# A perceiver block with a mixture of experts: the order of sixteen small matmuls in the attention's value products

## Chip, cores and metric

The kernel runs on one core of one Trainium2 chip, as one program. The metric is device time in microseconds of that core, the median of three runs. The profile is of one further execution of the same program.

## What is computed

One block of a perceiver: cross attention of 8 x 64 tokens onto 8 x 512 context rows, then causal self attention that is applied twice with a convolution between, then a mixture of 14 experts with two chosen per token. The part that matters here is the self attention:

```
qkv = x @ Wqkv_w.T + Wqkv_b
q, k, v = (qkv[:, :, 0], qkv[:, :, 1], qkv[:, :, 2])   # 16 heads of 32
ctx = _causal_attn(q, k, v)
conv_out = conv1d(ctx, conv_w, width 3) + conv_b
q2 = conv_out.reshape(b, s, 16, 32)
ctx2 = _causal_attn(q2, k, v)
out = ctx2 @ out_w.T + out_b
```

with _causal_attn: softmax of masked q k / sqrt(32), times v. There are 8 batches of 64 tokens, 512 features.

## The kernel before

The 512 tokens are cut into NT = 4 tiles of P = 128 rows, each of two batches (j = 0, 1) of S = 64 tokens. Each engine has its program written out by hand, and semaphores order them; nothing is moved by a scheduler. TensorE (the function under block.tensor) goes through the cross attention, then through eight attention steps m = 0 to 7: m = 0 to 3 are the four tiles in the first attention, m = 4 to 7 the same tiles in the second. In a step, `scores(m, half)` (line 1588) multiplies q and k per head, DVE takes the maximum and subtracts (lines 1070, 1071), ACT takes the exponential (581), DVE sums it (1078), POOL multiplies by the reciprocal (771), `values(m)` (1597) turns the probabilities on TensorE, ACT copies them to prT (589), and `outputs(m, w)` (1619) multiplies them with v. DVE's `take_out` (1092) adds the bias of v, writes the result and raises o_ready. Between these stand fills: projections of q, k and v (1535 to 1545) and the convolution (1555), placed by the table SLOTS. In the loop, step m runs `scores(m)`, `values(m - 1)`, `outputs(m - 1, 0)` and `outputs(m - 1, 1)`, with a fill after most of them. The last two steps stand after the loop in a list of their own (lines 1708 to 1746), mixed with the output projection `out_project` (1637), the turning of the normalised rows for the gate `turn_gate` (1384 by way of a helper), the gate's logits (1653), counts (1666, 1667) and the dispatch to the experts (1702). Then the experts' stage follows (1767 to 1769 for the first layer, 1790 for the second).

`outputs(m, w)` is called 16 times. One call makes 16 matmuls in fp32. H = 16 heads of DH = 32 features; HR = P // DH = 4. The head is h = 4(2 hp + w) + r. The stationary operand is v of one head and one batch: 64 rows (the key tokens, S) by 32 columns (the head's features). The moving operand is prT, the turned probabilities: 64 rows (key tokens) by 64 columns (query tokens). The result, 32 partitions by 64, goes to the partitions 32 r to 32 r + 31 of one PSUM bank, PO, at a column that follows from w, hp and j. So r says which strip of 32 columns of the array, and which 32 partitions of the bank, a matmul uses. w picks the rows of the array, the lower or the upper 64, and is the same within a call. With w = 0 a call waits for the turned probabilities (pT_ready) and until DVE has taken what the bank held before (o_ready); with w = 1 it waits for the matmuls of w = 0 (o_psum). The last matmul of each call raises o_psum; `take_out(m)` waits for both calls.

Of the kernel before, what the change touches and what calls it, by code (L numbers as in the profile page):

```python
# [31 lines left out]
HR = P // DH  # L32
# [16 lines left out]
def perceiver_kernel(nc, t, out):  # L49

    ctx = ExitStack()
    with ctx:
# [1325 lines left out]
        def _(pe):  # L1378
# [223 lines left out]
            def outputs(m, w):  # L1602

                n, u = m % NT, m % 2
                if w == 0:
                    pe.wait_ge(pT_ready, 2 * m + 2)
                    if m:
                        pe.wait_ge(o_ready, 2 * m)
                    if m < NT:
                        pe.wait_ge(vx_in[n], 32)  # L1610
                else:
                    pe.wait_ge(o_psum, 2 * m + 1)
                for hp in range(2):
                    for j in range(2):
                        for r in range(HR):
                            h = HR * (2 * hp + w) + r
                            v = vN if w == j else vX
                            at = 2 * P * w + P * hp + S * j
                            ins = mm(PO[DH * r:DH * (r + 1), at:at + S],
                                     v[S * w:S * (w + 1), n, DH * h:DH * (h + 1)],  # L1620
                                     prT[S * w:S * (w + 1), u, 4 * (r % 2) + 2 * (r // 2) + hp, S * j:S * (j + 1)],
                                     start=True, stop=True)
                ins.then_inc(o_psum, 1)
# [55 lines left out]
            for m in range(2 * NT - 2):  # L1679
                scores(m, 0)  # L1680
                fill(SLOTS[m][0])
                scores(m, 1)
                fill(SLOTS[m][1])
                if m:
                    values(m - 1)
                fill(SLOTS[m][2])
                if m:
                    outputs(m - 1, 0)
                fill(SLOTS[m][3])
                if m:  # L1690
                    outputs(m - 1, 1)
# [20 lines left out]
            values(before - 1)  # L1712
            fill(SLOTS[before][1])
            outputs(before - 1, 0)
            fill(SLOTS[before][2])
            turn_gate(0)
# [171 lines left out]
```

## Time and profile before

| | |
|---|---|
| median of 3 runs | 463.60 us (463.52 to 463.69) |
| profiled execution | 463.69 us |
| its span, first to last instruction | 461.9 us |
| TensorE matmuls busy | 434.2 us, 94% |
| VectorE busy | 277.5 us, 60% |
| ScalarE busy | 162.6 us, 35% |
| GpSimd busy | 50.4 us, 11% |
| mean granted clock of TensorE | 0.985 |

PE is TensorE's matmul side, PEld its weight loads, DVE VectorE, ACT ScalarE, POOL GpSimd. Each fp32 matmul appears as two matmul records and two weight loads. The end of a matmul record is modelled from its start: records of small matmuls overlap in the trace, and what counts is how far apart they start, or how long a group of them takes together. A record's own duration holds a fixed latency that lies beside the next ones. The granted clock is a share of 2.4 GHz. The chain of work that ended last is the profile's path back from the last instruction, with the time each piece added to it.

### The profile page before, as it was taken

The numbers are of one execution on the slowest core, as the hardware profiler recorded it, in microseconds if no ns is written. First come the engines' busy times: TensorE is split into PE (matmuls) and PEld (weight loads), VectorE is DVE, ScalarE is ACT, GpSimd is POOL, SyncE is SP. The second block draws the span as 40 slices with busy tenths as digits, with TensorE's granted clock in tenths as the row PEclk, the third lists the DMA queues.
The fourth block names the chain that finished last, engine by engine and source line by source line (L and its number), as shares of the span: only waits on it lengthen the run. The fifth ranks groups of instructions, "written<-read, shape, count | busy, mean of one in ns | idle before, by whom it ended". The sixth has DMA issues, their size and how long they took to land.

```text
span 461.9 us, 8060 instructions
## 1 busy us (share of the span) xinstructions
PE 434.2 (94%) x3103; PEld 312.0 (68%) x3112; DVE 277.5 (60%) x552; ACT 162.6 (35%) x316; POOL 50.4 (11%) x59
## 2 busy tenths in 40 slices
PE   1999999999999999999998999999999999999990
PEld 1666566688888899978567766666666656666660
DVE  5759697663544223389668866654456664445637
ACT  4335234114232114432326332455433355543100
POOL 1300000004221011110302300000000000000064
PEclk9999999999999999998989999999999999999996
DMA  7998794007999666005224669999999999984453
GB/s 263 406 390 324 261 415 178 1 1 270 405 406 403 247 241 241 1 3 203 81 89 178 199 203 376 352 325 339 335 338 362 380 323 341 340 320 142 171 151 122
DMA packets 52383, 116.95 MB, mean 253 GB/s; under 512 B 4835, under 2 KB 4851, under 8 KB 52353
## 3 DMA queue, kind: packets, MB, share of 16 engines
q1 hardware_dynamic: 25984, 67.12, 38.3%
q10 hardware_dynamic: 24800, 44.62, 27.5%
q0 software_dynamic: 1568, 4.79, 3.2%
q8 instruction: 21, 0.34, 0.3%
q14 instruction: 10, 0.07, 0.0%
HBM read 93.98 MB, written 21.50 MB: 250 GB/s over the span
## 4 chain that ended last, share of the span: by engine, by line
PE 87%; DVE 6%; DMA 2%; issue 2%; ACT 1%; POOL 1%; DVEq 0%; ACTq 0%; POOLq 0%
PE banks L1790 19%; PE banks L1555 10%; PE banks L1767 6%; PE banks L1769 6%; PE banks L1768 5%; PE banks L1416 4%; PE banks L1418 3%; PE banks L1403 3%; PE banks L1455 3%; PE banks L1417 3%; PE banks L1384 3%; PE banks L1637 3%; PE banks L1779 2%; PE banks L1588 2%; PE banks L1535 2%; PE banks L1597 2%
## 5 line engine op out<-in xcount | busy, mean ns | idle before, releaser
L1790 PE MATMUL banks<-w,A 128*128 128x512 f32 x208 | 91.6, 592 | 0.0
L670 ACT ACTIVATE A<-banks,b_sb 128x128 f32<-128x128 f32 x112 | 30.5, 384 | 111.0 <-issue 61.1
L1790 PEld LDWEIGHTS banks<-w,A 128*128 128x128 f32 x208 | 38.5, 190 | 43.1 <-issue 43.0
L1288 DVE COPY A<-banks 128x512 f32<-128x512 f32 x28 | 18.0, 686 | 66.9 <-PE banks L1769 66.7
L1216 DVE TENSOR_TENSOR w_lo<-w,w_hi 128x1024 fp32r<-128x1024 f32 x48 | 55.4, 1216 | 0.0
L603 ACT ACTIVATE w_hi<-w 128x1024 fp32r<-128x1024 f32 x48 | 47.3, 1095 | 0.8 <-ACT A L670 0.8
L1555 PE MATMUL banks<-A,w 128*128 128x128 f32 x384 | 46.6, 277 | 0.0
L1555 PEld LDWEIGHTS banks<-A,w 128*128 128x128 f32 x384 | 44.1, 192 | 0.8
L1767 PE MATMUL banks<-w_hi,xr 128*128 128x512 f32 x100 | 40.1, 401 | 0.6 <-DVE xr L1233 0.6
L1768 PE MATMUL banks<-w_lo,xr 128*128 128x512 f32 x104 | 40.5, 389 | 0.0
L1769 PE MATMUL banks<-w_hi,xr 128*128 128x512 f32 x100 | 39.0, 390 | 0.0
L809 POOL DMA_INDIRECT wqkv<-rows_dram,slot_i x8 | 7.6, 955 | 182.9 <-DMA rows_dram<-A 180.8
L771 POOL TENSOR_TENSOR A<-A,hrec 128x1024 f32<-128x1024 f32 x8 | 16.5, 2060 | 91.4 <-DVE hrec L1079 91.4
L1416 PE MATMUL banks<-w_lo,A2r 128*128 128x512 f32 x52 | 22.4, 430 | 2.1 <-DVE A2r L937 2.1
L1070 DVE TENSOR_REDUCE hmax<-banks 128x16 f32<-128x1024 f32 x8 | 9.8, 1222 | 22.0 <-PE banks L1588 22.0
L1768 PEld LDWEIGHTS banks<-w_lo,xr 128*128 128x128 f32 x104 | 19.6, 188 | 3.6
L1767 PEld LDWEIGHTS banks<-w_hi,xr 128*128 128x128 f32 x100 | 18.8, 188 | 4.2 <-DVE xr L1233 0.9
L581 ACT ACTIVATE A<-w 128x1024 f32<-128x1024 f32 x8 | 8.5, 1058 | 37.3 <-DVE w L1071 37.3
L1769 PEld LDWEIGHTS banks<-w_hi,xr 128*128 128x128 f32 x100 | 18.8, 188 | 4.0
L1418 PE MATMUL banks<-w_lo,A2r 128*128 128x512 f32 x52 | 21.1, 406 | 0.0
L1417 PE MATMUL banks<-w_lo,A2r 128*128 128x512 f32 x52 | 21.0, 404 | 0.0
L1535 PE MATMUL banks<-c_hi,w_lo 128*128 128x256 f32 x64 | 18.5, 289 | 0.5 <-DVE A2r L977 0.5
(288 smaller groups left out, 741.4 us busy)
## 6 DMA issues: line engine op xcount, KB each, us to landing
w<-in_w SPq DMA_DIRECT2D x12, 2048.0 KB, 10.4
w<-in_w ACTq DMA_DIRECT2D x12, 2048.0 KB, 10.4
rows_dram<-att ACTq DMA_DIRECT2D x1, 14592.0 KB, 42.8
A<-in_ctxT SPq DMA_DIRECT2D x8, 1024.0 KB, 10.3
A<-in_ctx SPq DMA_DIRECT2D x8, 1024.0 KB, 9.4
w<-in_w SPq DMA_DIRECT2D x6, 1024.0 KB, 5.8
rows_dram<-A ACTq DMA_DIRECT2D x13, 256.0 KB, 3.4
w<-in_wlT SPq DMA_DIRECT2D x3, 1024.0 KB, 15.1
```

The lines of the kernel that those rows point to most:

```text
L603: nc.scalar.activation(w1_hi[:, u, k * F:(k + 1) * F], w1[:, u, k * F:(k + 1) * F], ACT.Copy).then_inc(hi_ready, 1)
L670: ins = nc.scalar.activation(hT[:, u, f, :], HT[f // 4][:, tile(f % 4)], ACT.Gelu, bias=b1_sb[:, u, f:f + 1])
L1216: nc.vector.tensor_tensor(w1_lo[:, u, part], w1[:, u, part], w1_hi[:, u, part].bitcast(F32), ALU.subtract).then_inc(lo_ready, 1)
L1416: mm(Z[n][:, :], high[:, k, :], wl_hi[:, at, :], start=(part == 0 and k == 0), stop=False)
L1417: mm(Z[n][:, :], high[:, k, :], wl_lo[:, at, :], start=False, stop=False)
L1418: ins = mm(Z[n][:, :], low[:, k, :], wl_hi[:, at, :], start=False, stop=(part == 2 and k == KT - 1))
L1535: mm(onto, w_hi, c_hi[:, k, tokens], start=(k == 0), stop=False)
L1555: ins = mm(bank[:, tile(f)].rearrange("p (b s) -> p b s", b=2), conv[:, KT * tap + k, tile(f)], oT[:, k, 2 * n:2 * n + 2, tap:tap + S], st ...
L1767: mm(HP[u][c][:, :], xr[:, 0, u, k, :], high[:, at], start=(i == 0), stop=False)
L1768: mm(HP[u][c][:, :], xr[:, 0, u, k, :], low[:, at], start=False, stop=False)
L1769: ins = mm(HP[u][c][:, :], xr[:, 1, u, k, :], high[:, at], start=False, stop=(i == KT - 1))
L1790: ins = mm(YP[:, :], hT[:, u, f, :], w2[:, u, f * D:(f + 1) * D], start=(f == 0), stop=(f == FT - 1))
```

## The change

In `outputs` the three loops over hp, j and r are put in another order. Before, hp is outermost and r innermost; after, r is outermost, then hp, then j. The 16 matmuls, their operands, where each writes, the waits ahead of them and the semaphore that the last one raises are the same; every product is complete in one matmul (start and stop are both set), so no sum depends on the order.

```
-                for hp in range(2):
-                    for j in range(2):
-                        for r in range(HR):
-                            h = HR * (2 * hp + w) + r
+                for r in range(HR):
+                    for hp in range(2):
+                        h = HR * (2 * hp + w) + r
+                        for j in range(2):
                             v = vN if w == j else vX
                             at = 2 * P * w + P * hp + S * j
                             ins = mm(PO[DH * r:DH * (r + 1), at:at + S],
```

The order of r within a call is thus 0 1 2 3, four times over, before, and 0 0 0 0 1 1 1 1 2 2 2 2 3 3 3 3 after. (hp, j) runs through (0,0), (0,1), (1,0), (1,1), each for four matmuls before, and anew for each r after. No other engine's program is touched, and a call stands at the same place among TensorE's other work. The two places that the prediction speaks of, with each row an instruction or a run of equal ones (operands by the program's names, stationary x moving columns):

On TensorE, step 1 in the loop: its two calls (line 1619) between pieces of the convolution (1555) and of the next step.

```order
L1555 MATMUL banks<-A2,w1 128x128 [waits conv_in,pads_ready,o_ready,fill_taken]
L1555 MATMUL banks<-A2,w1 128x128 x11
L1619 MATMUL banks<-A2,A1 32x64 [waits vx_in1,o_ready,pT_ready]
L1619 MATMUL banks<-A2,A1 32x64 x15
L1555 MATMUL banks<-A2,w1 128x128 [waits conv_in,pads_ready,o_ready,fill_taken]
L1555 MATMUL banks<-A2,w1 128x128 x11
L1619 MATMUL banks<-A2,A1 32x64 [waits o_psum]
L1619 MATMUL banks<-A2,A1 32x64 x15
L1577 MATMUL banks<-causal_bf,ident_bf 128x512 [waits fill_taken,sub_ready]
```

These rows are the same before and after: what moves is which strip each of the sixteen uses, which the rows don't print.

On TensorE, after the loop: step 7's two calls, between an output projection and the gate, with what waits behind them.

```order
L1637 MATMUL banks<-w2,cT 128x512 x3
L1619 MATMUL banks<-A2,A1 32x64 [waits o_ready,pT_ready]
L1619 MATMUL banks<-A2,A1 32x64 x15
L1619 MATMUL banks<-A2,A1 32x64 [waits o_psum]
L1619 MATMUL banks<-A2,A1 32x64 x15
L1653 MATMUL banks<-gate,cT 128x14 [waits lg_taken,sub_ready,cT_ready]
L1653 MATMUL banks<-gate,cT 128x14 x3
L1384 MATMUL banks<-ident,cn 128x128 [waits cT_ready,normed]
```

Here too the rows stay where they are, and only the order inside the two groups of sixteen is another.

## Rows read from the trace of the kernel before

**Rows 1.** The page's parts 1 and 2: TensorE busy, and granted clock.
```profile
PE 434.2 (94%) x3103; PEld 312.0 (68%) x3112; DVE 277.5 (60%) x552; ACT 162.6 (35%) x316; POOL 50.4 (11%) x59
...
PEclk9999999999999999998989999999999999999996
```
**Rows 2.** TensorE's waits from 130 to 262 us: total, times, longest.
```profile
PE banks L1702 <- DVE att L1138: 1.1, 1, 1.1
PE banks L1767 <- DVE xr L1233: 0.8, 1, 0.8
PE banks L1577 <- issue: 0.8, 5, 0.2
PE banks L1577 <- DVE lgc L1107: 0.5, 1, 0.5
PE banks L1384 <- DVE cn L837: 0.5, 1, 0.5
PE banks L1597 <- POOL A L771: 0.3, 1, 0.3
```
**Rows 3.** The chain that ended last: start us, us added, what.
```profile
149.93 0.58 PE banks L1619 x32
...
233.37 3.51 PE banks L1637 x4
...
236.97 1.82 PE banks L1637 x4
```
**Rows 4.** Line 1619, all records: duration ns min/median/max, first and last start, form.
```profile
L1619 PEld LDWEIGHTS banks<-A x512: 102/107/107, 137.4 to 230.8; 64*32 64x32 f32 x171
L1619 PE MATMUL banks<-A x512: 216/216/241, 137.4 to 230.9; 64*32 64x64 f32 x171
...
L1619 PE MATMUL banks<-A 64*32 64x64 f32 x512 | 10.4, 219 | 0.3
```
**Rows 5.** Timeline of one call, cut at 149.92 (both), 149.96 and 150.30.
```profile
149.86 0.26 PE L1619 MATMUL banks<-A 64*32 64x64 f32 x4
149.86 0.15 PEld L1619 LDWEIGHTS banks<-A 64*32 64x32 f32 x8
149.86 0.32 PE L1619 MATMUL banks<-A 64*32 64x64 f32 x8
149.86 0.65 PE L1619 MATMUL banks<-A 64*32 64x64 f32 x32
```
**Rows 6.** The chain in the experts' stage: wide fp32 matmuls.
```profile
263.81 6.87 PE banks L1790 x16
```
**Rows 7.** The chain around step 5's second call.
```profile
212.43 0.61 ACT cT L455
...
213.08 1.08 PE banks L1653 x8
```
**Rows 8.** TensorE's timeline, steps 5 to 7: start, us, line, count [idle before].
```profile
212.32 0.65 PE L1619 MATMUL banks<-A 64*32 64x64 f32 x32
...
222.45 1.39 PE L1619 MATMUL banks<-A 64*32 64x64 f32 x64
...
224.24 1.09 PE L1597 MATMUL banks<-ident,A 128*128 128x128 f32 x8 [0.27 <-POOL A L771]
...
229.71 1.39 PE L1619 MATMUL banks<-A 64*32 64x64 f32 x64
...
232.62 0.70 PE L1384 MATMUL banks<-ident,cn 128*128 128x128 f32 x4 [0.52 <-DVE cn L837]
```
**Rows 9.** DVE's timeline at step 7's take_out.
```profile
232.48 0.75 DVE L1092 TENSOR_TENSOR cT<-banks,qkv_b 128x256 f32<-128x256 f32 x2
```
**Rows 10.** Two windows (us, busy and count by engine, granted clock), then step 4's calls.
```profile
216.03:219.44 3.41, 3.41 (x41) 2.78 (x31) 3.12 (x5) 0.80 (x2) 0.00 (x0) 0.50 1.02 407
233.10:236.51 3.41, 3.35 (x6) 1.32 (x5) 1.66 (x11) 2.49 (x3) 0.00 (x0) 0.50 0.02 7
...
195.31 1.39 PE L1619 MATMUL banks<-A 64*32 64x64 f32 x64
```

## The prediction, made before the changed kernel had run

> **What bounds the kernel now.** Read the page's first two parts first: TensorE is busy 94% of the span, at close to its full clock [rows 1]. Next the waits of TensorE alone, over the stretch in which the changed function runs and up to the experts: it waits for other engines five times, 3.2 us in all, and only three of these waits, 1.3 us, lie between the first and the last of the changed calls (line 1577 for DVE, 1384 for DVE, 1597 for POOL) [rows 2]. So in this stretch TensorE sets the end, and time added to it is time added to the kernel, unless it falls into one of those three waits or beside another engine's step. The chain of work that ended last says the same: a call of `outputs` stands in it with all its 32 records and 0.58 us [rows 3].
>
> **What the change moves.** Nothing is added or removed: 16 calls (8 steps m, w = 0 and 1) of 16 matmuls, which the trace shows as 512 matmul records and 512 weight loads, two of each per fp32 matmul, 64 rows by 32 columns, 64 elements streamed [rows 4]. What changes is which of them stand next to each other. The four values of r write the partitions 0, 32, 64 and 96 onwards, that is, four different column strips of the array. Before, r runs innermost: neighbours lie on four different strips. After, r runs outermost: the eight records of one strip (four matmuls, two records each) stand in a row, then those of the next strip.
>
> **What a strip costs per record.** I read one call closely. Cut off at later and later moments, its matmul row counts x4 at 149.92, x8 at 149.96, x32 at 150.30 [rows 5]. The records start in fours, and from x8 to x32, six fours, 0.34 us pass: 0.056 us for a turn of four (the cuts are 0.01 us wide; 0.053 to 0.06 is in them). What is a turn? The wide fp32 matmul shows the streaming price: 16 records of 512 elements in 6.87 us [rows 6], so 0.429 us for 512, 0.84 ns an element, and 64 elements need 0.054 us. So a turn is just one record's streaming time, and in it four records ran, one on each strip, side by side. Alone on its strip, a record takes the whole turn. The order after therefore leaves one strip working while three stand still.
>
> **The sum per call.** Before: 8 turns plus about 0.13 us of fixed time at the ends = 0.58 us [rows 3]. After, eight records on each of four strips in succession. Where the strip changes, the next record needs no free turn of its own: it can start beside the last one of the strip before, as neighbours on different strips do now. So 4 x 8 - 3 = 29 turns: 21 more, 21 x 0.056 = 1.18 us per call. Two bounds: if a change of strip does not overlap, 32 turns, +1.34 us; and if the four strips went on working together whatever the order, +0. I take 1.18, since the records of the call that is traced do start side by side as soon as the strips differ. 16 x 1.18 = 18.9 us.
>
> **The weight loads.** The second record on a strip needs a load that must be hidden behind the first one's streaming. The loads run ahead now: at 149.92 the row of loads counts x8 where that of the matmuls counts x4 [rows 5]; the first four pairs fill all four strips, so loads 5 to 8 are second loads onto strips on which a matmul is under way. A load of 32 columns is short: where only 14 elements are streamed, 8 records with loads of 128 columns take 1.08 us [rows 7], 0.135 each, so a quarter of the columns is about 0.034 us, below the 0.056 of a turn. I take the loads at nothing, hidden by the stream of the record before. If that cover were gone, each turn would be 0.056 + 0.034 = 0.09 us, a call 29 x 0.09 + 0.13 = 2.74 us, 2.16 us more than now, and 16 calls 34.6 us.
> The Trainium skill, "TensorE: Matmul & The Clock Gate", section "Part 3: Packing small matmuls — row/col tiling", says that a weight load overlaps matmuls in flight only when its row group differs; within a call all loads have the same row group, so by that sentence the cover would be gone. The same page, in its Part 2, also lets a load go ahead into the background weight buffer, and the counts just quoted side with that.
>
> **Where the time lands.** Steps m = 0 to 4, 10 calls: TensorE waits for no engine there (what stands as "issue" before line 1577, five times, stays) [rows 2], all on the chain: 10 x 1.18 = 11.8 us. Step 5: w = 0 stands before a convolution piece and counts in full, 1.18. Its w = 1 starts at 212.32, beside ACT's copy of the turned rows (212.43 to 213.04), for which the gate's matmuls at 213.08 wait [rows 7, 8]; against the usual 0.58 from the start of a call to the next matmul it is 0.76, so 0.18 is absorbed: +1.0. What is late next is the gate, and the choice on DVE that line 1577 waits for comes after it, so that wait of 0.5 us stays. Step 6 (222.45, both w): the 0.27 us until POOL's probabilities [rows 2, 8] go: 2.36 - 0.27 = +2.09. Step 7 (229.71, both w): DVE normalises beside it, and 0.52 us of waiting for it goes [rows 2, 8]: +1.84. DVE's `take_out` comes after these calls and moves with them, but only the gate's matmuls, about 1.1 us as in [rows 7], and a turn lie between it and its reader, out_project(3), and its two operations take 0.76 us [rows 9], so it stays covered. Later waits (line 1702 and 1767 for DVE) follow from matmuls that all shift, so I let them be. Sum: 11.8 + 1.18 + 1.0 + 2.09 + 1.84 = 17.9 us. The experts' stage is TensorE's own and starts that much later; its transfers come no later relative to it.
> The profiled execution took 463.69 us (span 461.9 and 1.8 around it), the median of the runs is 463.60. 463.69 + 17.9 = **481.6 us**.
>
> **The clock.** It stands at half, 1.2 instead of 2.4 GHz, in two stretches, 216.03 to 219.44 and 233.10 to 236.51 [rows 10]. Before each fall TensorE had run a call of `outputs` or two, the gate's 14-element matmuls and, before the first, the scores' small ones, and had waited 0.5 and 0.52 us [rows 2, 8]. Half clock over matmuls on the chain costs half of its own length, 1.7 us: the second stretch holds the first half of out_project(3), 3.51 us for four records where the next four take 1.82 [rows 3]. The first costs little, as ACT, DVE and POOL stand in the chain behind it. The change lengthens the calls before such falls and takes one of the two waits away, so it can go either way.
>
> **Rivals.**
> (a) The clock falls after the lengthened pairs at steps 0, 4 and 6 too (1.39 + 2.36 = 3.75 us each, one strip of four at work), as it does after step 7 now. Two or three new stretches of half clock: +3.4 to +5.1, 485 to 487 us; with one more 488. For it: both present falls follow such work. Against: from 195.3 to 198.6 a pair of calls [rows 10] stands beside a pair of scores, and the clock stayed. Chance 0.3.
> (b) The waits at 224 and 232 go and with them the second half-clock stretch, -1.7: 479.9 us. This is inside my forecast's own case.
> (c) A change of strip does not overlap: 16 x 3 x 0.056 = +2.7, 484.3 us. Chance 0.07.
> (d) Loads uncovered, as above: 463.69 + 34.6 - 1.0 = 497 us. Chance 0.07.
> (e) The change doesn't do what it says: TensorE starts matmuls of free strips ahead of queued ones, and the calls stay at 0.58 us. 463.6 us. All records in the trace start in program order, but the order now never gives it cause to do otherwise. Chance 0.03.
> (f) Faster: the same overtaking, and DVE's and POOL's timing shifts enough that the half-clock stretch at 233 (1.7 us) is gone: 463.7 - 1.7 = 462.0 us. It decides only where the 16 calls grow by less than 1.7 us together, 0.1 us each, a tenth of one strip's extra. Chance 0.01.
>
> **How the numbers follow.** The forecast (29 turns, loads hidden, clock as now or one half-clock stretch fewer) has 0.52: 479 to 483 us. With (a) and (c) the range goes up to 488; (d), (e) and (f), 0.11, stay outside, with the tails of the rest. Range 478.8 to 488. Faster by over 0.2% (0.9 us, about what a measurement can tell from no change): 0.01; within: 0.03; slower: 0.96.
>
> **What would show it.** Right: the row of line 1619 about 1.75 us a call instead of 0.58 before the next matmul, its counts rising by one each 0.056 us; busy time of these matmuls from 10.4 [rows 4] to near 30 us; waits at lines 1597 and 1384 gone; DVE's wait for line 1619 longer. A call near 1.9 us speaks for (c), near 2.7 for (d), near 0.6 for (e); (a) would show as more half-clock stretches right after the pairs. I would be wrong if the experts' stage changed length, or if the calls grew and the span did not.

## The result and the profile after

| | before | changed |
|---|---|---|
| median | 463.56 us (462.59 to 463.69, 4 runs) | 470.27 us (469.85 to 471.29, 4 runs) |
| ratio | | 1.0162, 95% interval 1.0134 to 1.0191 |
| span of the profiled execution | 461.9 us | 469.1 us |
| mean granted clock | 0.985 | 0.993 |

The change costs 6.7 us. The direction was forecast, the size was not: 481.6 us, with a range from 478.8, was far too much. Of the executions below, one of the kernel with two strips at a time took 1133.63 us and is left out of its ratio; nothing on record explains it.

The page of the changed kernel, its span, part 1 and the clock row of part 2, to be held against [rows 1]:

```profile
span 469.1 us, 8060 instructions
...
PE 442.1 (94%) x3103; PEld 322.1 (69%) x3112; DVE 277.8 (59%) x552; ACT 162.6 (35%) x316; POOL 50.3 (11%) x59
...
PEclk9999999999999999999999999999999999999997
```

TensorE's matmuls are 7.9 us longer busy and its weight loads, which lie beside them, 10.1; no other engine's time has moved by more than 0.3, and the two dips of the clock row are gone: the second thing to explain, beside the calls.

One call of step 1 between two convolution pieces (TensorE's timeline), and the whole group of line 1619, which was [rows 4]:

```profile
151.50 1.39 PE L1619 MATMUL banks<-A 64*32 64x64 f32 x32
152.82 2.94 PE L1555 MATMUL banks<-A,w 128*128 128x128 f32 x24
...
L1619 PE MATMUL banks<-A 64*32 64x64 f32 x512 | 22.3, 219 | 1.0 <-PE banks L1619 0.9
```

A call takes 1.32 us to the next matmul, not 0.58 as before and not the 1.75 of the forecast: +0.74. Its row lasts 1.39 us, and the last record in it 0.216 us [rows 4], so from the first start to the last 1.17 us pass; before it was 0.65 - 0.216 = 0.43 [rows 5]. This is the measure used below. Both calls and group agree: 22.3 - 10.4 = 11.9 us, 0.74 a call.

The same call cut off at later and later moments, as in [rows 5] (151.60, 151.66, 151.71, 151.76 and 151.81):

```profile
151.50 0.30 PE L1619 MATMUL banks<-A 64*32 64x64 f32 x2
151.50 0.35 PE L1619 MATMUL banks<-A 64*32 64x64 f32 x3
151.50 0.41 PE L1619 MATMUL banks<-A 64*32 64x64 f32 x4
151.50 0.49 PE L1619 MATMUL banks<-A 64*32 64x64 f32 x6
151.50 0.52 PE L1619 MATMUL banks<-A 64*32 64x64 f32 x7
```

Up to x4 the records start one at a time, 0.056 us apart: a single strip. Between 151.71 and 151.76 two start, and from there they come closer together than a turn. Strip 0 has eight records, and only five have started at 151.76; the sixth of the row is strip 1's first. So the next strip begins long before the first has started all of its own. (The rows don't name the strip; this is read from the counts and from the order of the program.)

Where TensorE's timeline stands later than before, in us: the first call 0.2 (137.55), the scores of step 5 after ten calls 7.5 (204.70), the gate of tile 0 8.9 (221.93), the last `values` 8.7 (232.98), the calls of step 7 8.2 (237.95), out_project(3) 9.5 (242.91), the counts in the middle of it 7.9 (244.63), and at the end 7.2. The ten calls of steps 0 to 4 bring it all; the six of steps 5 to 7 bring 4.4 and the same stretch gives back more. TensorE's waits between 130 and 262 us, against [rows 2]:

```profile
PE banks L1577 <- issue: 1.3, 6, 0.5
PE banks L1702 <- DVE att L1138: 1.1, 1, 1.1
PE banks L1619 <- PE banks L1619: 0.9, 1, 0.9
PE banks L1767 <- DVE xr L1233: 0.8, 1, 0.8
PE banks L1597 <- POOL A L771: 0.3, 1, 0.3
```

The wait of line 1384 for DVE is gone, as forecast. That of 1597 for POOL has stayed, and so has that of 1577 for DVE: it is the longest of the six under `issue`, 0.53 us at 223.51. The one of 1619 for 1619, 0.9 us between the two calls of step 7, is new. The other five under `issue`, 0.2 us each before line 1577, are none, here and in [rows 2]: the line has two matmuls, of which those timelines show one. A record that is missing reads like a wait; in the profile of the kernel of the first experiment both records are there at 204.40, and no such wait.

### The profile page after: what moved, and what is told of

It reads as the page before. It is cut to its first block, busy times and chain, and to the rows that moved or that the text cites. A ratio compares the mean times of both kernels' runs of the same rounds, so it can differ in the third digit from the quotient of the medians.

```text
span 469.1 us, 8060 instructions
## 1 busy us (share of the span) xinstructions
PE 442.1 (94%) x3103; PEld 322.1 (69%) x3112; DVE 277.8 (59%) x552; ACT 162.6 (35%) x316; POOL 50.3 (11%) x59
## 4 chain that ended last, share of the span: by engine, by line
PE 88%; DVE 6%; DMA 2%; issue 2%; ACT 1%; POOL 1%; DVEq 0%; ACTq 0%; POOLq 0%
PE banks L1790 19%; PE banks L1555 10%; PE banks L1767 6%; PE banks L1769 5%; PE banks L1768 5%; PE banks L1619 4%; PE banks L1416 3%; PE banks L1418 3%; PE banks L1403 3%; PE banks L1417 3%; PE banks L1455 3%; PE banks L1384 3%; PE banks L1779 2%; PE banks L1637 2%; PE banks L1588 2%; PE banks L1535 2%
## 5 line engine op out<-in xcount | busy, mean ns | idle before, releaser
L1416 PE MATMUL banks<-w_lo,A2r 128*128 128x512 f32 x52 | 22.5, 433 | 2.1 <-DVE A2r L937 2.1
L1619 PE MATMUL banks<-A 64*32 64x64 f32 x512 | 22.3, 219 | 1.0 <-PE banks L1619 0.9
L1619 PEld LDWEIGHTS banks<-A 64*32 64x32 f32 x512 | 19.7, 106 | 4.7 <-issue 2.0
L1418 PE MATMUL banks<-w_lo,A2r 128*128 128x512 f32 x52 | 21.1, 406 | 0.0
## 6 DMA issues: line engine op xcount, KB each, us to landing
w<-in_w SPq DMA_DIRECT2D x12, 2048.0 KB, 10.2
w<-in_w ACTq DMA_DIRECT2D x12, 2048.0 KB, 11.3
```

The costliest lines, as they stand in the source:

```text
L1416: mm(Z[n][:, :], high[:, k, :], wl_hi[:, at, :], start=(part == 0 and k == 0), stop=False)
L1418: ins = mm(Z[n][:, :], low[:, k, :], wl_hi[:, at, :], start=False, stop=(part == 2 and k == KT - 1))
L1619: ins = mm(PO[DH * r:DH * (r + 1), at:at + S], v[S * w:S * (w + 1), n, DH * h:DH * (h + 1)], prT[S * w:S * (w + 1), u, 4 * (r % 2) + 2 * ( ...
```

## Experiments

### New order in steps 0 to 4, and in steps 5 to 7

```
-                for hp in range(2):
-                    for j in range(2):
-                        for r in range(HR):
+                for hp, j, r in (strips_first if m <= 4 else strips_last):
```

strips_first is the list of the new order, strips_last that of the old one; the second kernel has m >= 5.

> The new order (r outermost) only in steps 0 to 4, ten of the sixteen calls; the old one in steps 5 to 7. In the changed kernel a call takes 1.32 us from its start to the next matmul against 0.58, +0.74. Theory 1: the loss sits in these ten calls, on the chain with nothing to hide it, and the two half-clock stretches of before stay, because steps 5 to 7 are as before: +7.4 us, 471.0 us, clock 0.985. Rival: the half-clock stretches depend on when the work falls and not on the calls of steps 5 to 7; with everything 7.4 us later they vanish or move here too: about 469 us, clock 0.993.

Measured: 470.5 us, ratio 1.015 (1.0123 to 1.0178) to 463.4 beside it: +7.1 us, clock 0.986 to 0.988. The profile has its half clock in one stretch of 6.8 us here, with the windows before and after it at full:

```profile
216.00:223.30 7.30, 6.88 (x137) 5.86 (x135) 6.66 (x16) 1.63 (x5) 0.00 (x0) 1.00 0.35 104
223.30:230.12 6.82, 6.75 (x57) 4.40 (x47) 5.00 (x9) 3.31 (x4) 0.00 (x0) 0.50 0.89 354
```

The two stretches of before have become one of twice the length. Theory 1 is right on the ten calls: 7.4 expected from 10 x 0.74, 7.1 measured, nothing hidden. Making everything 7 us later does not by itself free the clock.

> The new order only in steps 5 to 7, the complement. Theory 1: six calls at +0.74 = +4.4 us of TensorE time, of which most lies beside waits for ACT, POOL and DVE, and the two half-clock stretches go with it: -0.5 us net, 463.1 us, clock 0.993. Rival: the stretches vanished by timing alone; here they stay, and the six calls cost what the waits of 1.0 us leave: +3 us, 466.6 us, clock 0.985. The gap of 0.86 us between the two calls of step 7 comes again if it belongs to this order at this place.

Measured: 463.88 us (462.2 to 467.54, 10 runs), ratio 1.0018 (0.999 to 1.0047): no difference that can be told. What can be told is inside it. Its executions fall apart by their mean clock: five at 0.992 to 0.994 took 462.2 to 463.23 us, two at 0.990 464.53 and 465.3, three at 0.982 to 0.985 took 465.92 to 467.54. At full clock (median 462.79) the six longer calls cost nothing that can be told: the time is 0.6 us below that of before, within the spread of both; with the clock as before (median 466.22) they cost 2.5 to 4.1 us. The clock is worth some 3.4 us here. The profiled execution is one with 0.990; it has one stretch at half clock, behind the longer calls of step 5:

```profile
217.99:221.35 3.36, 3.36 (x41) 3.02 (x42) 3.04 (x6) 0.32 (x1) 0.00 (x0) 0.50 1.03 412
```

So the longer calls don't always hold the clock. The executions of the changed kernel fall apart in the same way: of 13 executions in all, 11 at 0.993 or 0.994 took 469.85 to 471.3 us and two at 0.985 and 0.986 took 472.97 and 473.26. There it is worth some 2.7 us (median of the eleven 470.41). The gap between the calls of step 7 was not there in the kernel with only steps 5 to 7 changed.

### Two matmuls in a row on a strip, and two strips at a time

```
+                for hp, j, r in [(hp, j, r) for hp in range(2) for r in range(HR) for j in range(2)]:
```

and

```
+                for hp, j, r in [(hp, j, r) for g in range(2) for hp in range(2) for j in range(2)
+                                 for r in (2 * g, 2 * g + 1)]:
```

> All sixteen calls in the order hp, r, j: two matmuls, four records, in a row on each strip, strips in turn. Theory 1: TensorE starts a matmul record on a free strip ahead of at most three records that have not started. Worked through record by record with 0.056 us per record on a strip (0.080 the first) this gives 0.435 us from the first to the last start for the old order and 1.178 for the new one, as measured, and 0.65 us here: +0.22 a call, 3.5 us in all, some 0.3 of it hidden, 466.7 us. Rival: neighbouring strips overlap by a fixed time, 0.2 us as in the changed kernel: a run of four records, 0.25 us, would then be nearly hidden by it, about 0.48 us a call, under +1 us. Rival: no overtaking, 1.48 us a call, +15 us.

> All sixteen calls with strips 0 and 1 alternating for eight matmuls, then strips 2 and 3. Theory 1 (overtaking at most three unstarted records): 0.79 us from the first to the last start, +0.36 a call, 5.8 us in all, some 0.5 hidden or given back: 468.8 us. Rival with a fixed overlap of 0.2 us at the one change of strips: 0.71 us a call, +4.4, 467.6 us. Rival without overtaking: 1.08 us a call, +10.

Measured: 463.95 us, ratio 1.001 (0.9991 to 1.003), and 466.09 us, ratio 1.0063 (1.0038 to 1.0088). The call of step 1 w = 0 in each timeline:

```profile
150.39 0.69 PE L1619 MATMUL banks<-A 64*32 64x64 f32 x32
```

```profile
150.54 0.90 PE L1619 MATMUL banks<-A 64*32 64x64 f32 x32
```

Less the 0.216 us of the last record, 0.47 and 0.68 us. Theory 1 of these two (at most three unstarted records passed over; not the theory 1 of the first two experiments) said 0.65 and 0.79 and falls, and with it the idea of one count of records that may be passed over. The rival with a fixed overlap said 0.48 and 0.71, nearer but off in the second. What fits is something else, **theory 2**: records are handed out in program order and quickly; each strip has a queue of its own, for three records beside the one that runs; handing out stops where the next record's queue is full. Four records in a row on a strip just fit, so two in a row cost almost nothing; with eight, the hand-out stands until the fifth has started, and only then reaches the next strip, 0.25 us after the first. With a turn of 0.056 us (the first 0.080) and 0.0033 us per record handed out, counted through record by record, this gives 0.436 us for the old order, 1.170 for the new one, 0.456 for two in a row and 0.681 for two strips; measured 0.43, 1.17, 0.47 and 0.68. With room for two, the same counting gives 1.34 for the new order and 0.68 for two in a row; with room for four, 1.00 for the new order: only three fits. The 0.0033 us can be read in the kernel with two in a row: its row counts x3 when cut at 150.42 and x4 at 150.44, four strips reached 0.013 us apart, where in the old order the four start 0.007 apart, one fp32 matmul being two records on the same strip.

```profile
150.39 0.27 PE L1619 MATMUL banks<-A 64*32 64x64 f32 x3
150.39 0.28 PE L1619 MATMUL banks<-A 64*32 64x64 f32 x4
```

### Two forecasts of theory 2: three in a row, and the scores

Theory 2 was made from four orders, so it had to forecast others.

```
+                for hp, j, r in ([(i // 2, i % 2, r) for r in range(HR) for i in range(3)]
+                                 + [(1, 1, r) for r in range(HR)]):
```

> All calls with three matmuls (six records) in a row on each strip, then one matmul on each. Theory 2 (a queue of three per strip): strip 1 starts right after strip 0's third record, at 0.139 us, and the last start comes 0.834 us after the first. Theory 1 (at most three unstarted records passed over in all): 0.874 us; no overtaking: more than 1.4 us. Total under theory 2: +0.4 a call, 6.4 us, less what is hidden, 468 to 470 us.

Measured in one execution: 469.02 us, and the call:

```profile
150.81 1.06 PE L1619 MATMUL banks<-A 64*32 64x64 f32 x32
```

1.06 - 0.216 = 0.84 us, against 0.834 by theory 2 and 0.874 by the limit of three records in all.

The other forecast is at another line with another shape, `scores`, whose matmuls use 32 rows by 64 columns:

```
-                for c in range(KT):
-                    for b in range(2):
-                        r = 2 * half + b
-                        for j in range(2):
+                for b in range(2):
+                    r = 2 * half + b
+                    for j in range(2):
+                        for c in range(KT):
```

> The calls of outputs in the old order; instead the 16 matmuls of each half of the scores (32 rows by 64 columns each) are put in an order in which the four on one piece of the array stand in a row (b, j, c in place of c, b, j). Theory 2, formed from the two-in-a-row and two-strips kernels: records are handed out in program order, one each 0.0033 us, and each piece of the array has a queue of its own for three waiting records beside the running one; handing out stops when the next record's queue is full. It gives 0.436, 1.170, 0.456 and 0.681 us from the first to the last start for the four orders run so far (measured 0.435, 1.175, 0.472, 0.682), and here about 1.17 to 1.2 where the old order has 0.46: +0.73 a half, 16 halves, 11.7 us; some of it hidden or given back in steps 5 to 7, 472 to 475 us. Rival: the queues belong to column strips alone and pieces above one another share one: longer than that, up to 1.7 us a half. Rival: small pieces in 32 rows are started ahead without a limit: no change.

Measured in two executions: 478.51 us, ratio 1.0318 (1.029 to 1.0347), +14.8 us, more than expected. The first half of the scores of step 0 on TensorE's timeline (0.69 us in the kernel before):

```profile
115.69 1.54 PE L1588 MATMUL banks<-A 32*64 32x64 f32 x32
```

1.54 less the record's 0.217 is 1.32 us, 0.85 more than the 0.69 - 0.217 = 0.47 of before. The first turn on a piece is longer here, 0.107 us, perhaps as the load of 64 columns stands before it, and the others are 0.058; with these theory 2 gives 1.31. I had put in the turn of the other shape. One queue shared by pieces side by side, in the same rows, is out: the same counting gives 1.42 us at the least. For pieces above one another, in the same columns, this order can't tell: their records lie so far apart that a shared queue gives 1.31 too. What speaks against that one is the order of before, measured at 0.47: a shared queue that starts its records strictly in turn would make it 0.57, one that doesn't would give 0.47 as well. 16 halves at 0.85 are 13.6 us; the rest may lie with the clock, which stood at half for 10.2 us between 200 and 260 us instead of 6.8.

### Matmuls in the waits

What makes the clock fall in steps 5 to 7? The first try puts two mask matmuls (bf16, 128x512) ahead of the calls of step 7:

```
+                    if m == 2 * NT - 1:
+                        for i in range(2):
+                            mm(PO[:, :], ident_bf[:, :], causal_bf[...], start=True, stop=True)
```

> The old order, with two mask-sized matmuls (bf16, 128x512, 0.21 us each) into the result bank ahead of the calls of step 7, where TensorE waits 0.52 us for DVE soon after; their result is overwritten by the calls. Theory: the half-clock stretch at 233 us costs 1.6 us of the chain and comes after small matmuls and waits; with full-sized ones in the place of the wait it goes, and the kernel takes 462.0 us, 1.5 less than before, clock 0.989. Rival: the stretch stays, and the two matmuls are hidden in the wait: 463.5 us, clock 0.986.

Measured: 463.36 us, ratio 0.9991 (0.9974 to 1.0009). No gain; the profile still has two stretches at half clock, from 224.4 and from 234.7 us:

```profile
224.39 1.97 PE L1597 MATMUL banks<-ident,A 128*128 128x128 f32 x8 [1.76 <-POOL A L771]
...
233.85 0.66 PE L1384 MATMUL banks<-ident,cn 128*128 128x128 f32 x4
```

Both rows say something. The first stretch stands 8 us later than in [rows 10], right behind a wait of 1.76 us, though TensorE's program up to there is that of before: its place differs from one execution to the next. And the wait of 0.52 us at line 1384 is gone, hidden by the two matmuls, and the clock fell all the same. The second try puts them into the waits themselves:

```
+            def spare(n):
+                pe.wait_ge(out_taken, n - 1)
+                for i in range(2):
+                    mm(FB[(len(FILLS) + n) % 2][:, :], ident_bf[:, :], causal_bf[...], start=True, stop=True)
...
             gate_logits(0)
+            spare(2)
             scores(last, 0)
...
             gate_logits(1)
+            spare(3)
             turn_gate(2)
```

The bank is the one that the next output projection overwrites.

> The old order, with spare full-sized matmuls put into the two waits of TensorE in steps 5 to 7: two (bf16, 128x512, 0.21 us each, 0.43 together) behind the gate's logits ahead of the scores of step 7 (wait 0.53 us) and two ahead of the turn of tile 2 (wait 0.52 us), into a bank that the output projection overwrites. In executions of one kernel those with a mean clock of 0.993 are 2.6 to 3.5 us shorter than those with 0.985. Theory: the half-clock stretches follow these waits and small matmuls; filled, the clock holds: 460.7 us, 2.8 less than before, clock 0.993. Rival: two are too little, as in the kernel with two ahead of step 7's calls: 463.5 us, clock 0.986.

> As the kernel with two spare matmuls in each wait, with four in each, 0.85 us, 0.33 us longer than each wait. Theory: if the clock holds, 2.8 us less and at most 0.7 us more, 461.4 us, clock 0.993. Rival: the clock falls as before and the spare matmuls cost what the waits don't hide: 464.2 us, clock 0.986.

Measured: 461.97 us with two, ratio 0.9946 (0.9928 to 0.9963); 462.0 us with four, ratio 0.9966 (0.9943 to 0.9989). Windows of the kernel with two, ahead of and over the places where [rows 10] shows half the clock (granted clock is the third number from the end):

```profile
212.00:216.00 4.00, 3.83 (x70) 2.81 (x73) 3.50 (x10) 1.63 (x5) 0.00 (x0) 1.00 0.50 156
216.03:219.44 3.41, 3.32 (x72) 2.40 (x65) 3.02 (x8) 1.08 (x2) 0.00 (x0) 1.00 1.02 406
...
233.10:236.51 3.41, 3.31 (x15) 1.57 (x13) 2.55 (x15) 2.49 (x3) 0.00 (x0) 1.00 0.01 2
```

The clock holds, here and everywhere else between 200 and 260 us, and this kernel is faster than both: 2.3 us less than the one before beside it. Expected were 2.8. Two of its four executions had a mean clock of 0.989, and of the ten with four spare matmuls eight stood at 0.991 to 0.993 and two at 0.984 and 0.987 (465.93 and 463.43 us), where the kernel before beside them stood at 0.985 to 0.987 in eleven of thirteen. So the fall is made rarer, not impossible. A wait alone doesn't decide: TensorE waits 1.76 us for POOL in it, at the last `values` and behind the calls of step 6, and no fall follows, where behind the same wait in the kernel of the first try it did:

```profile
224.89 1.09 PE L1597 MATMUL banks<-ident,A 128*128 128x128 f32 x8 [1.76 <-POOL A L771]
```

Whether the spare matmuls work through the clock and nothing else is asked by the changed kernel with the same two in each wait.

> The new order in all calls together with the two spare matmuls in each of the two waits. Theory: the spare matmuls gain only by keeping the clock, which the changed kernel holds anyway (0.993); so nothing more is gained: 470.3 us, as the changed kernel. Rival: they gain 1.5 to 2.3 us by something else, as they did in the old order: 468.0 to 468.8 us.

Measured: 470.9 us, ratio 1.0144 (1.0123 to 1.0166), clock 0.993: nothing gained where the clock is full already. That the spare matmuls work through the clock stands; what makes the clock fall is not shown by it. The spare matmuls of the old order and the longer calls of the new one buy the same thing, so it cannot be had twice.

### The changed kernel once more

> The changed kernel once more, beside the kernel before on the same chip. Expected: +6.7 to +7.2 us, clock 0.993 in most executions and no half-clock stretch between 200 and 250 us in the profile. The gap of 0.86 us between the two calls of step 7 was absent where only steps 5 to 7 had the new order, so it should be absent here if it is a matter of one execution, and present if it belongs to this kernel.

Measured: 470.54 us, ratio 1.0164 (1.013 to 1.0197). Its calls of step 7 and what follows, on TensorE's timeline:

```profile
237.96 2.84 PE L1619 MATMUL banks<-A 64*32 64x64 f32 x64
240.73 1.06 PE L1653 MATMUL banks<-gate,cT 128*128 128x14 f32 x8
241.65 0.64 PE L1384 MATMUL banks<-ident,cn 128*128 128x128 f32 x4
242.12 1.88 PE L1637 MATMUL banks<-w,cT 128*128 128x512 f32 x4
```

No gap between the two calls, and out_project(3) 0.8 us earlier than in the first profile. The gap belongs to one execution; what made it was not found. The clock is full again: the four records of out_project(3) take 1.7 us on the chain, where [rows 3] has 3.51.

## Why the prediction was wrong

**What bounds the kernel: right.** TensorE sets the end in steps 0 to 4, and the ten calls there came through in full, 7.1 of 7.4 us.

**The turn: right.** 0.056 us for a record alone on its strip is what the changed kernel shows, and that the loads are hidden is right too: no turn of `outputs` in any order was longer, after the first. Rival (d) is out. The Trainium skill ("TensorE: Matmul & The Clock Gate", "Part 3: Packing small matmuls — row/col tiling") lets a load overlap matmuls in flight only where its row group differs. The trace doesn't agree: all 32 loads of a call have the same one, and the records of a strip still started 0.056 us apart.

**The sum per call: this step failed.** It said that one strip works while three stand still, 4 x 8 - 3 = 29 turns, +1.18 us. Measured +0.74. The step took it that TensorE starts no record of a strip before all earlier records of other strips have started, save the last. The experiments show three waiting places per piece of the array instead: the next strip begins after the fifth of eight, some 4.5 turns after it, so 3 x 4.5 + 8 = 21.5 turns pass and not 29. Of the 11.3 us by which the forecast was off, 16 x 0.44 = 7.0 come from here, and most of the rest from the clock, below.

**What I could have read.** Rival (e) says that the order now never gives TensorE cause to start a record ahead of an earlier one. It does. Each fp32 matmul is two records on the same strip, so the program's order was 0 0 1 1 2 2 3 3, and [rows 5] has four started at once at 149.92 and four more a turn later. Strip 3's first record had to pass the second ones of strips 0, 1 and 2. The rows had the queues in them, and I read the fours as the order of the program. My bounds, +0 and +1.34, held the truth, but the range was built around one end, and overtaking had a chance of 0.04 in (e) and (f) together. ([rows 9] has 0.75 us for DVE's two operations, where the prediction says 0.76; nothing hangs on it.)

**Steps 5 to 7 and the clock: half right.** The forecast had 1.18 + 1.0 + 2.09 + 1.84 = 6.1 us from them, with the larger calls, less 1.7 if the second half-clock stretch went (b). At 0.74 a call, 4.4 us minus the 1.0 I let the waits absorb, they would be 3.5; the executions with the old clock show 2.5 to 4.1, so that part held. The clock was mis-sized: I counted only the second stretch at half, 1.7 us, since ACT, DVE and POOL stand behind the first. Both together are worth some 3.4 us in the kernel with new order in steps 5 to 7, some 2.7 in the changed one, and in most executions of the changed kernel both go. The first one is not free: at half clock TensorE reached the calls of step 6 with nothing to spare (222.45, the wait for POOL 0.27), at full clock it needs 4.46 us from the turning of step 6's probabilities to them (225.23 to 229.69) where it had needed 5.82, and the longer calls of step 6 fall into that. This is why the wait for POOL at line 1597 stayed at 0.31 where I had it gone: with +2.09 forecast for step 6, nothing was added. The chain that ended last runs there through DVE, ACT and POOL, which don't know of the new order (its `issue` pieces of 0.02 to 0.07 us between these are left out):

```profile
227.09 1.24 DVE w L1071
228.34 1.07 ACT A L581
229.43 1.23 DVE hsum L1078
230.69 0.26 DVE hrec L1079
231.02 1.91 POOL A L771
232.98 1.09 PE banks L1597 x8
```

**Rival (a): out.** Neither profile of the changed kernel has a stretch at half clock after the lengthened pairs, or anywhere before the last matmuls, and a mean of 0.993 or 0.994 in 11 of 13 executions leaves room for none. In the other two the clock fell at a place that no profile shows.

**Added up.** Steps 0 to 4 +7.1 (measured alone), steps 5 to 7 at full clock -0.6 (measured alone): 6.5, and 6.7 to 6.9 measured together. Of the 11.3 us of the miss, the sum per call is 7.0 and the clock 2.7 to 3.4; 0.9 to 1.6 are left, 0.3 of them in steps 0 to 4. The last matmuls of the experts start 7.90 us late in the first profile (439.62 against 431.72) and the end is 7.2 late: 0.7 us come back behind all matmuls, where POOL, DMA and DVE collect the result. Why they do is open, and so is why the changed kernel keeps the clock in nearly all executions and the one with only steps 5 to 7 changed in half of them.

## What to carry to other kernels

Let neighbouring small matmuls lie on different pieces of the array, but without being strict: two fp32 matmuls in a row on a piece cost 0.04 us per sixteen, four in a row 0.74. Before costing an order, write down the order of the records (two per fp32 matmul) and hold it against the starts in the trace: a start out of order shows how far the engine looks ahead. Small matmuls with short waits among them can cost several times the wait by way of the clock, and two full-sized matmuls of no use, put into each of two such waits, were worth 2.3 us. Where they stand matters: two of them ahead of step 7's calls, which hid one of the waits as well, gained nothing.

## What the runs showed of the hardware

What fits all runs: small records of TensorE are handed out in program order, 0.0033 us each, to queues of three, one for each piece of the array (64 x 32, and by the forecast that held 32 x 64 too, with the reservation made there on pieces above one another). Seven cases, five orders of one shape and two of the other, agree to 0.02 us a call; four of them made the theory. Two records on one piece start 0.056 us apart at full clock, 64 fp32 elements streamed; those on different pieces 0.007 us in the order of before, where two records are handed out from one piece to the next.

The granted clock fell to half (1.2 GHz) in steps 5 to 7, after small matmuls and waits of about 0.5 us. It stayed at 2.4 GHz in 11 of 13 executions of the changed kernel (by their mean of 0.993 or 0.994) and more often than before with bf16 matmuls of 0.21 us each in the two waits. But it fell in the kernel with only steps 5 to 7 changed, behind the longer calls of step 5 (217.99), and with the 0.52 us wait gone (234.7). A wait of 1.76 us behind the calls of step 6 was followed by a fall in one kernel and by none in another. What decides was not settled.
